# The same calls in another hand-written order: a four-chain transformer kernel on one core

## The reference, cut to what matters

```python
h = _layernorm(x) * (1 + ca) + sa
x = x + ga * encoder(h)                 # 4 layers, below, then a last layernorm
h = _layernorm(x) * (1 + cb) + sb
x = x + gb * moe(h)
# one layer
h = layernorm(x); q, k, v = h @ Wq + bq, h @ Wk + bk, h @ Wv + bv
qp, kp = elu(q) + 1, elu(k) + 1
attn = (qp @ (kp^T v)) / (qp @ sum(kp) + 1e-6)      # per head, 16 heads of 8
x = x + attn @ Wo + bo
x = x + relu(layernorm(x) @ W1 + b1) @ W2 + b2
# mixture
probs = softmax(h @ router); coef = the two largest of each token, else 0
out = sum_e coef_e * (silu(h @ gate_e) * (h @ up_e)) @ down_e + shared expert
```

## Time and profile before

| what | value |
|---|---|
| median of three runs | 582.92 us (582.63 to 583.69) |
| profiled execution | span 581.6 us; no other time is listed for it, so the median lies 1.3 us above its span |
| TensorE matmul busy | 558.9 us, 96% |
| TensorE weight load | 532.6 us, 92% |
| VectorE, ScalarE, GpSimd busy | 437.6, 398.4, 261.8 us (75, 69, 45%) |
| share of TensorE in the chain that ended last | 87% |
| ScalarE table loads | 23, of 1283 ns each |

### The profile page before, as it was taken

The page is one execution under the profiler, slowest core; times in us unless marked ns, Lnnn a source line. Parts: engine busy times, 40 slices in busy tenths (PEclk is TensorE's granted clock), DMA queues, the critical chain, the costliest instruction groups (busy, mean ns, idle before and its releaser), DMA issues.

```text
span 581.6 us, 13216 instructions
## 1 busy us (share of the span) xinstructions
PE 558.9 (96%) x4572; PEld 532.6 (92%) x4572; DVE 437.6 (75%) x1543; ACT 398.4 (69%) x1395; POOL 261.8 (45%) x431
## 2 busy tenths in 40 slices
PE   6899999999999999999999999998999999999997
PEld 3588998998999999998999999998999999999896
DVE  5868677777986777777996777768897676667795
ACT  2888698886766766686585666687676666666651
POOL 4353566654323446654503446556404244355420
PEclk9999999999999999999999999999999999999999
DMA  7700523100000000000000000000000000000000
GB/s 228 214 5 0 201 50 115 68 1 2 20 2 19 1 2 2 1 2 2 2 20 20 1 2 1 1 2 2 2 19 20 2 2 1 2 2 1 2 19 18
DMA packets 11049, 15.60 MB, mean 27 GB/s; under 512 B 960, under 2 KB 8224, under 8 KB 10600
## 3 DMA queue, kind: packets, MB, share of 16 engines
q1 hardware_dynamic: 8904, 12.54, 6.9%
q0 software_dynamic: 448, 1.25, 0.8%
q10 hardware_dynamic: 1632, 0.98, 0.6%
HBM read 12.63 MB, written 2.14 MB: 25 GB/s over the span
## 4 chain that ended last, share of the span: by engine, by line
PE 87%; DVE 4%; ACT 4%; POOL 3%; issue 1%; ACTq 1%; DVEq 0%; POOLq 0%
PE psA L1612 21%; PE psB L1612 20%; PE psC L1612 20%; PE psD L1612 18%; PE psC L1684 1%; PE psB L1684 1%; PE psA L1684 1%; PE psD L1684 1%; PE psC L1735 1%; PE psD L1735 1%; PE psB L1735 1%; PE psA L1735 0%; ACT H L491 0%; POOL xA L839 0%; POOL rstdC L841 0%
## 5 line engine op out<-in xcount | busy, mean ns | idle before, releaser
L841 POOL TENSOR_TENSOR rstdA<-msA,neghalf 128x2 f32<-128x2 f32 x20 | 14.3, 716 | 68.6 <-ACT eqkA L468 65.4
L841 POOL TENSOR_TENSOR rstdD<-msD,neghalf 128x2 f32<-128x2 f32 x20 | 14.0, 698 | 58.6 <-ACT ziD L468 52.7
L1612 PE MATMUL psA<-w,H 128*128 128x128 f32 x256 | 33.1, 275 | 0.0
L1612 PE MATMUL psC<-w,H 128*128 128x128 f32 x256 | 33.1, 275 | 0.0
L1612 PE MATMUL psD<-w,H 128*128 128x128 f32 x256 | 32.4, 275 | 0.0
L1612 PE MATMUL psB<-w,H 128*128 128x128 f32 x256 | 31.8, 275 | 0.0
L1612 PEld LDWEIGHTS psA<-w,H 128*128 128x128 f32 x256 | 31.0, 192 | 0.0
L1612 PEld LDWEIGHTS psC<-w,H 128*128 128x128 f32 x256 | 30.9, 192 | 0.0
L1612 PEld LDWEIGHTS psD<-w,H 128*128 128x128 f32 x256 | 30.6, 192 | 0.0
L1612 PEld LDWEIGHTS psB<-w,H 128*128 128x128 f32 x256 | 30.3, 192 | 0.0
L468 ACT ACTIVATE eqkA<-xA 128x129 f32<-128x129 f32 x64 | 19.4, 308 | 15.6 <-DVE xA L1196 9.9
(11 more groups left out here) (588 smaller groups left out, 2384.7 us busy)
## 6 DMA issues: line engine op xcount, KB each, us to landing
M<-modulation_rows SPq DMA_DIRECT2D x2, 1280.0 KB, 8.2
M<-modulation_rows SPq DMA_DIRECT2D x1, 2560.0 KB, 8.7
out<-X SPq DMA_DIRECT2D x16, 128.0 KB, 1.9
M<-in_attn_W SPq DMA_DIRECT2D x3, 256.0 KB, 4.0
X<-in_attn_x_in ACTq DMA_DIRECT2D x2, 256.0 KB, 3.5
M<-in_attn_W ACTq DMA_DIRECT2D x1, 256.0 KB, 3.6
wo<-in_attn_Wo POOLq DMA_DIRECT2D x1, 256.0 KB, 4.7
wm<-in_wmod SPq DMA_DIRECT2D x1, 256.0 KB, 4.2
```

The source lines that it names most:

```text
L841: pool.tensor_tensor(b.rstd[:, :], b.ms[:, :], neghalf[:, :], ALU.pow).then_inc(b.s_rstd.sem, 1)
L1612: return pe.matmul(o, lhsT, rhs, start=start, stop=stop)
```

## The change

Every call keeps its body, its semaphores and its count. Their order in the four lists differs, in the opening, in the round, and at the seam between rounds:

- TensorE: `out_project` and `out_project2` of a chain get more of the other chains' calls between them; `expand`, `contract` and `transposes` of the pairs are interleaved differently; the experts of A go ahead of those of B; the loop begins later in the chains' work (at `expand(B, i, 0, 1)`), so that a round's last calls are the next round's first `project_keys`, `sums` and `attend` of C and D.
- ScalarE, VectorE and GpSimd: the same kind of reordering.
- Opening: `first_rows` stands in the order B, A, D, C on TensorE and B, A, C, D on VectorE; two waits count accordingly. On VectorE `first_rows(B)` stands ahead of `parameters`.

The core of the diff (TensorE around layer 0, the last layer and the experts; VectorE and GpSimd where the text below refers to them):

```diff
+ENTRY_PE = (1, 0, 3, 2)
+ENTRY_DVE = (1, 0, 2, 3)
...
-                dve.wait_ge(s_inmod, b.c + 1)
+                dve.wait_ge(s_inmod, ENTRY_PE.index(b.c) + 1)
...
-                    dve.wait_ge(s_factor, b.c + 1)
+                    dve.wait_ge(s_factor, ENTRY_DVE.index(b.c) + 1)
```

```diff
 # VectorE, opening
+            in_stats(D_, 0)
             in_stats(C, 0)
+            in_stats(A, 0)
             in_stats(B, 0)
-            in_stats(A, 0)
-            in_stats(D_, 0)
+            first_rows(B)
             parameters()
-            fold_matrix(0)
-            fold_matrix(1)
             first_rows(A)
...
+            divided(A, 0, 0)
+            bias_low(1)
+            modulation(3)
             positive_keys(B, 0, 0)
-            divided(A, 0, 0)
+            modulation(4)
+            scale(C, 0, 1)
+            move(A, 0, 1)
             positive_queries(B, 0, 0)
             masked(B, 0, 0)
 # TensorE, opening
             condition()
+            first_rows(B)
             first_rows(A)
-            first_rows(B)
             parameters()
-            first_rows(C)
             bias_rows(0)
             first_rows(D_)
+            first_rows(C)
...
             sums(A, 0, 0)
+            attend(A, 0, 0)
             project_keys(B, 0, 0)
             project_queries(B, 0, 0)
-            attend(A, 0, 0)
-            sums(B, 0, 0)
-            attend(B, 0, 0)
             out_project(A, 0, 0)
             fold_weights(2)
+            out_project2(A, 0, 0)
+            sums(B, 0, 0)
+            transposes(D_, 0, 0)
+            attend(B, 0, 0)
```

```diff
 # TensorE, round
+                out_project(D_, i, 0)
...
-                attend(D_, i, 0)
                 contract(B, i, 0, 0)
+                transposes(A, i, 2)
                 contract(B, i, 0, 1)
-                out_project(D_, i, 0)
-                transposes(A, i, 2)
                 transposes(C, i, 1)
                 out_project2(D_, i, 0)
...
                 out_project(D_, i, 3)
+                logits(A, i)
+                transposes(C, i, 7)
                 out_project2(D_, i, 3)
-                transposes(C, i, 7)
-                logits(A, i)
                 expand(C, i, 3, 0)
                 expand(C, i, 3, 1)
                 transposes(D_, i, 7)
                 logits2(A, i)
+                contract(C, i, 3, 0)
+                gate(A, i, 2)
+                up(A, i, 2)
+                logits(B, i)
                 expand(D_, i, 3, 0)
                 expand(D_, i, 3, 1)
-                logits(B, i)
...
+                coef_transposes(A, i)
                 contract(C, i, 3, 1)
                 coef_transposes(B, i)
-                coef_transposes(A, i)
+                spread(A, i, 0)
+                gate(A, i, 1)
                 spread(B, i, 0)
                 gate(B, i, 1)
-                spread(A, i, 0)
-                gate(A, i, 1)
+                up(A, i, 1)
```

```diff
 # GpSimd, round
                 shift_out(B, i)
                 rstd(D_, i, 8)
+                rstd(B, i, 10)
+                add_bias(C, i, 8)
                 add_bias(D_, i, 8)
-                rstd(B, i, 10)
 # VectorE, round
                 weights(CD, i)
                 gate_up(D_, i, 0)
+                if i + 1 < STEPS:
+                    positive_keys(B, i + 1, 0)
+                    positive_keys(A, i + 1, 0)
                 gate_up(C, i, 0)
                 if i + 1 < STEPS:
+                    positive_queries(A, i + 1, 0)
+                    masked(A, i + 1, 0)
                     positive_queries(B, i + 1, 0)
                     masked(B, i + 1, 0)
-                    positive_keys(A, i + 1, 0)
                 weigh(D_, i, 0)
```

More of the change, by code:

```diff
@@ L980, in _ @@
                 shift_out(D_, i)
-                add_bias(C, i, 8)
+                rstd(D_, i, 10)
                 gated(C, i)
@@ L1437, in _ @@
-                scale(A, i, 5)
+                low_part(C, i, 3)
                 move(B, i, 4)
-                low_part(A, i, 4)
+                positive_keys(A, i, 2)
                 move(D_, i, 3)
-                low_part(C, i, 3)
+                positive_queries(A, i, 2)
                 scale(B, i, 5)
-                positive_keys(A, i, 2)
+                masked(A, i, 2)
+                move(C, i, 4)
                 low_part(B, i, 4)
-                positive_queries(A, i, 2)
-                masked(A, i, 2)
+                divided(A, i, 2)
@@ L1460, in _ @@
                 move(D_, i, 4)
-                low_part(C, i, 4)
+                low_part(A, i, 5)
+                positive_keys(C, i, 2)
+                scale(D_, i, 5)
                 move(B, i, 5)
-                low_part(A, i, 5)
-                scale(D_, i, 5)
+                positive_queries(C, i, 2)
+                masked(C, i, 2)
                 low_part(D_, i, 4)
-                positive_keys(C, i, 2)
-                positive_queries(C, i, 2)
+                move(A, i, 6)
+                divided(C, i, 2)
+                low_part(B, i, 5)
+                scale(A, i, 7)
                 positive_keys(D_, i, 2)
-                masked(C, i, 2)
-                low_part(B, i, 5)
-                divided(C, i, 2)
-                move(A, i, 6)
                 if i + 1 < STEPS:
@@ L1547, in _ @@
                 stats(D_, i)
+                weigh(A, i, 0)
                 weigh(B, i, 0)
-                weigh(A, i, 0)
+                scale_last(D_, i)
+                gate_up(A, i, 1)
+                gate_up(B, i, 1)
                 leave(C, i)
-                gate_up(B, i, 1)
-                scale_last(D_, i)
+                stats(C, i)
                 weigh(B, i, 1)
-                stats(C, i)
-                gate_up(A, i, 1)
+                low_part(D_, i, 8)
                 weigh(A, i, 1)
@@ L1587, in _ @@
                     masked(A, i + 1, 0)
-                    divided(B, i + 1, 0)
+                    positive_queries(B, i + 1, 0)
+                    masked(B, i + 1, 0)
+                weigh(D_, i, 0)
+                if i + 1 < STEPS:
+                    divided(A, i + 1, 0)
                 weigh(C, i, 0)
@@ L1606, in _ @@
                 finish(C, i, 1)
+                if i + 1 < STEPS:
+                    low_part(C, i + 1, 0)
+                    positive_keys(D_, i + 1, 0)
+                    positive_queries(D_, i + 1, 0)
+                    move(B, i + 1, 1)
+                    positive_keys(C, i + 1, 0)
+                    positive_queries(C, i + 1, 0)
+                    masked(C, i + 1, 0)
+                    masked(D_, i + 1, 0)
+                    divided(C, i + 1, 0)
+                    low_part(B, i + 1, 1)
+                    move(A, i + 1, 2)
+                    divided(D_, i + 1, 0)
         @block.tensor
@@ L1924, in _ @@
                 out_project2(A, i, 1)
-                expand(D_, i, 0, 1)
+                transposes(C, i, 2)
+                attend(B, i, 1)
                 contract(D_, i, 0, 0)
+                contract(D_, i, 0, 1)
                 out_project(B, i, 1)
-                contract(D_, i, 0, 1)
-                transposes(C, i, 2)
+                project_keys(C, i, 1)
+                transposes(A, i, 3)
+                project_queries(C, i, 1)
                 out_project2(B, i, 1)
@@ L1932, in _ @@
                     fold_weights(7)
[L1933 to L1935 removed]
                 expand(A, i, 1, 0)
+                sums(C, i, 1)
+                expand(A, i, 1, 1)
                 transposes(D_, i, 2)
[L1938 to L1939 removed]
+                attend(C, i, 1)
+                transposes(B, i, 3)
+                contract(A, i, 1, 0)
+                contract(A, i, 1, 1)
+                expand(B, i, 1, 0)
+                out_project(C, i, 1)
                 project_keys(D_, i, 1)
                 project_queries(D_, i, 1)
[L1942 to L1945 removed]
+                out_project2(C, i, 1)
+                expand(B, i, 1, 1)
+                contract(B, i, 1, 0)
                 sums(D_, i, 1)
[L1947 to L1948 removed]
+                transposes(A, i, 4)
+                contract(B, i, 1, 1)
                 attend(D_, i, 1)
[L1950 to L1956 removed]
                 transposes(C, i, 3)
@@ L2116, in _ @@
                 if i + 1 < STEPS:
-                    attend(B, i + 1, 0)
-                    sums(A, i + 1, 0)
+                    attend(A, i + 1, 0)
                 spread(C, i, 0)
```

678 lines of the change are left out of this document (331 added, 347 removed).

## The result

The changed kernel takes 598.22 us (median of 4 runs, 597.48 to 599.12) against 583.0 us (582.63 to 583.69) on the same chip: a ratio of 1.0263, 95% interval 1.0249 to 1.0278. It is 15 us slower, where 2.3 us faster was forecast; a round takes 139.1 us, past the 136 us that the prediction gave as its sign of being wrong. The profiled execution has a span of 595.6 us against 581.6.

A forecast was written before the change was run, and what follows sets the result against it. TensorE, busy 96% of the span, was taken as the bound, so only its idle time could change. Terms: -6.0 + 4 x 0.2 + 3 x 0.3 + 2.0 = -2.3 us, from 582.9 to 580.6 us; range 575.5 to 586.

The forecast's parts named there:

- the 136 us: Full round: 134.5 to 135 us was expected; 136 or more would mean no layer gain or experts giving back more.
- laying out VectorE's operations in the new order with the lengths of this round: Experts of A and B: hand layout using profiled durations; route some 0.2 us earlier, logits(C) 0.1 to 0.3 us later.
- Layers, -1.5 each: Four layer stages: more TensorE work between dependent calls removes stalls, -1.5 us each, between -1.9 and -0.8.
- Round 0, experts_low: GpSimd's 2.90 us operation in round 0: TensorE's 1.45 us stall stays, 0; -1.45 to +1.0 possible.
- Experts of A and B, +0.2 each: Experts of A and B, four rounds: gains waited for again at up(A) and logits(C); net +0.2 us, between -0.8 and +0.8.
- The move of `rstd(B, 10)` ahead of `add_bias(D, 8)`: GpSimd at the experts' entry: rstd(B, 10) no longer waits behind that call, shortening chain B's last norm by 0.4 us.
- the three holes: Experts' entry on TensorE: idle 0.26 to 0.66 us each at out_project2(D), expand(C) and logits2(A), to be filled by other calls.
- Opening, +2.0: Opening: first_rows(B) ahead of parameters and later VectorE delays cost +2.0 us, between +0.5 and +3.5.
- Experts of C and D, +0.9: Experts of C and D with the seam: VectorE delays against removed seam stalls, +0.3 us three times, each -0.5 to +1.2.
- End, 0: Last 20 us: order of the last gates changes but the waits don't, 0.
- The slower one: Rival, chance 0.22: VectorE bounds the experts, idling 1.4 us more per round behind a late ScalarE result; 586.2 us.
- that rule at one place: Shared-port lock at round 0's experts_low: two-input scale would be caught, making the sum about 1 us higher.

The follow-up runs named there:

- mix_layers_thin: Kernel before with the changed order in the layers alone on all four engines, and add_bias cut to one column of 128: 579.08 us, ratio 0.9924.
- after_thin: Changed kernel with GpSimd's add_bias cut to one column of 128, the rest of the bias left out: 584.89 us.
- mix_layers: Kernel before with the changed order in the layers alone, on all four engines, all work done: 590.72 us, ratio 1.0131.
- after: The changed kernel itself, set against the kernel before: 598.22 us, ratio 1.0263.
- after_fill: Changed kernel with each add_bias replaced by a GpSimd pow of 128x2 elements that takes as long: 583.51 us, ratio 1.0024.
- after_open: Changed kernel with parameters back ahead of first_rows(B) on VectorE: 597.74 us.
- after_elow: Changed kernel with round 0's experts_low moved back behind add_bias(B, i, 6) on GpSimd: 598.81 us.
- after_hold: Changed kernel with seven more GpSimd waits per round, so wide operations start only after that chain's scale or scale_last is done: 596.09 us.
- before: The kernel without the change, against which the changed kernel is measured: 583.0 us.
- after_split: Changed kernel with each add_bias as two operations of 128x128 instead of one of 128x256: 590.59 us.
- after_pieces: Changed kernel with every wide GpSimd operation cut into pieces of 128x128: 589.57 us, ratio 1.0101.
- mix_split: Kernel before with the changed order in the layers alone, each add_bias in two halves and experts_low in ten pieces: 587.32 us, ratio 1.0068.
- mix_pick: Kernel before with the changed order in only three parts of each layer stage, and experts_low in ten pieces: 602.05 us.

## Why the prediction was wrong

**The step that failed** is one that runs through two terms: "laying out VectorE's operations in the new order with the lengths of this round". The lengths belonged to the order. A `scale` of 0.42 us is one that meets no wide GpSimd operation; in the new order 24 of 64 meet one and take 0.53 us or more, before 4 of 64. The sum also had no term for TensorE's clock, which the prediction read as 1.00 throughout.

**Layers, -1.5 each.** Measured +2.9, +1.0, +0.9, +0.3. The TensorE side of the step was right in kind: the stalls named at `out_project2(D)` and `out_project2(B)` are gone, and without the wide `add_bias` a stage gains 0.8 to 1.2 us in mix_layers_thin and up to 1.7 in after_thin, inside the -1.9 to -0.8 given. What was missed is the holding, up to 2.5 us in each of rounds 1 and 2 (mix_layers +1.4, mix_layers_thin -1.1), or 2.1 to 2.2 where GpSimd's time stays the same (after against after_fill).

**Round 0, experts_low.** The earlier trace rows was read rightly as a VectorE operation that waits for GpSimd's, and the text even named which operations would stand in its time. It took 0 and gave +1.0 as the upper bound. Measured: the stage of round 0 costs 2.1 us more than that of round 1 in mix_layers (3.5 against 1.4), and 1.9 in the changed kernel, for two reasons. The operation was caught 0.7 us into the 2.9 instead of 1.3, and TensorE's wait was 1.87 us instead of 1.28 by the same view. And TensorE's clock fell behind the longer wait, which took 1.6 us, most of the difference.

**Experts of A and B, +0.2 each.** Measured +1.5 on average. Most of it is holding. Two `add_bias` hold `scale_last(B)`: the wait at `logits(B)` was to shrink by 0.6 to 0.8 us, and TensorE waits 0.83 us there. Without it (after_fill) the stage loses 0.7 us less. `gated(D)` and `shift_out(D)` hold `weights(AB)`. In round 2 of after_fill `shift_out(D)` starts at 416.88 us, behind the last product of `weights(AB)` for B at 416.61, which then takes 0.17 us instead of 0.74 to 0.76; there the stage loses 0.3 us, in the other three rounds 0.9. So 0.7 and 0.6 of the 1.6 us are holding, and at most 0.3 is left for the order itself. The move of `rstd(B, 10)` ahead of `add_bias(D, 8)`, which was booked as a gain of 0.4 us, made the first: before, the `add_bias` was over when `scale_last` started. As to the three holes that the change seemed to fill, the one at `expand(C)` is still there, 0.67 us from start to start where it was 0.52, since on ScalarE `squares(B, i, 9)` stands ahead of `transposed(C, i, 7)`. VectorE's list was laid out by hand, ScalarE's was not.

**Opening, +2.0.** Right in size (+2.4; 2.8 between the groups). TensorE did stand empty from 7.9 to 8.85 us and `transposes(A, 0, 0)` came 1.0 us later, as the prediction said, but taking the cause away (after_open) gave nothing back; what the step costs is shown, why it does stays open. **Experts of C and D, +0.9.** Near: +0.7. **End, 0.** Right: +0.1.

**The rivals.** The slower one (VectorE becomes the bound of the experts, 586.2 us) had the right engine and the wrong cause: not a result that arrives late for its turn, but operations that last longer. It was priced at 1.4 us per round in the experts, and 1.5 came, but the layers were left at their gain.

The Trainium skill's page "SBUF — State Buffer" (section "SBUF: two separate sides") gave the mechanism: whichever of a VectorE operation with two SBUF inputs and a GpSimd operation starts first has the shared pair for the whole instruction. The prediction weighed that rule at one place, for 1 us. The runs agree with it where an `add_bias` starts just ahead of a `scale`: 0.89 us for the `scale` beside 0.69 us of `add_bias`, 0.66 us where the `add_bias` comes in two halves. They differ from its words in one point: a `scale` that starts 0.07 us into a 128x2 pow of 0.69 us takes 0.42 us, so what counts is not GpSimd's whole instruction there.

## What to carry to other kernels

A duration read from a trace holds for the neighbours that it had. Before an order is changed, list for each wide GpSimd operation which VectorE operations that read SBUF alone may run beside it; the collision seen in every round here is the pair in which GpSimd releases a VectorE operation and goes straight on to wide work. Cutting GpSimd's wide operation into pieces bounded the loss to about one piece here, while a wait in front of it moved the loss to GpSimd's own readers. And a stall between two calls may be the cover of the third: ask what stands behind it before filling it.

## What was not expected of the hardware

TensorE's granted clock fell to its lower level behind single waits of 1.9 us in round 0 (after, after_elow, after_hold, after_open, mix_layers) and did not behind those of 1.3 to 1.7 us at the same place (before, after_fill, after_thin, after_split, after_pieces). The length of one wait doesn't decide alone. One of 1.9 us, in mix_split, was not followed by a fall; that kernel had its fall in the opening (0.84 of full from 20 to 30 us). And in mix_pick the clock fell at 77.9 us, behind two waits of 0.87 and 1.03 us with one pair of transposes between them. In the changed kernel the fall cost 1.6 us, nearly as much as the wait.

Runs of one kernel can differ by such a fall: after_thin's two groups lie 4.6 us apart (clock 0.999 and 0.991), and single runs of after_fill (588.2 us, 0.991) and after_split (596.2 us, 0.989) lie about 5 us above their medians. Where in the execution these runs lost their clock isn't known, since no trace of them was kept.

The opening varies from run to run by more than its parts: with the same list `fold_weights(0)` starts anywhere within 1.1 us (opening of the change) or 1.7 us (opening of before), and all that follows moves with it.
